# Up weights kept in DRAM, an earlier choice for the second half, and three shared jobs moved behind the routed ones

## Chip, cores and metric

The kernel runs on one core of one Trainium2 chip. The metric is the device time of one execution in microseconds (us). TensorE (PE) multiplies matrices; VectorE (DVE), ScalarE (ACT) and GpSimd (POOL) do the rest, and SyncE (SP) issues most DMAs.

## Reference

x has 32 sequences x 256 tokens x 128 channels, 8192 token rows in all. It goes through a mixture-of-experts layer, a retention layer and the same mixture of experts again:

```python
x = x + 0.5 * ffn(layernorm(x))          # called layer 1 below
x = x + attn(layernorm(x))               # retention, 16 heads
x = x + 0.5 * ffn(layernorm(x))          # called layer 2 below

def ffn(x):                              # xf: 8192 rows of 128
    shared = gelu(xf @ Wfc_s + bfc_s) @ Wproj_s + bproj_s        # hidden size 512
    probs = softmax(xf @ Wr)                                     # 8 experts
    topk_p, topk_i = top_k(probs, 2); topk_p /= sum(topk_p)
    routed = sum over e of gate[:, e] * (gelu(xf @ Wfc[e] + bfc[e]) @ Wproj[e] + bproj[e])
    return shared + routed
```

All is float32. The kernel multiplies in a faster format: each operand is split into a rounded part (`hi`) and the rest (`lo`), and three products hi*hi, hi*lo and lo*hi are summed.

## The kernel before

All 64 blocks of 128 token rows stay in SBUF (`x`). An expert layer works in two halves of 32 blocks. Rows are normalised into `xn`; logits and the two best experts of each row are found; each row gets a slot in `x_slots`, a buffer in DRAM sorted by expert.

**Jobs.** The matrix work is a list of 56 jobs per layer, each of 512 rows (`job_order`): first 16 shared jobs (no choice needed, rows straight from `xn`), then 20 routed jobs of half 0, then 20 of half 1. In each half 4 of the 20 are pair jobs, 256 rows for each of two experts. A position in this list is called job i; the code counts layers from 0. TensorE's program for job i (`tensor_jobs`) is `up(i)`, `turn(i+1)` (transposes of the next job's rows, L353), `back(i-2)` (y back to rows, L402), `down(i-1)` and then `tensor_between(i)`. ScalarE does y of job i-2, the four GELUs of job i, x_hi of job i+1 (`take_x`), the rows and the store of job i-2 (`take_rows`, L521), and `scalar_between(i)`. VectorE does x_lo of job i+1 (`split_x`), the update of x by job i-2 if it is shared, the two splits of h (`split_h`), and `vector_between(i)`. Each engine works its program strictly in this order.

**Choice and placing.** `choose_and_place` is a generator of small VectorE steps that ends in `slot` (L733). For half 0 it runs ahead of the jobs. For half 1 its steps are spread over jobs: `ROUTING_STEPS` says how many run at the end of which job. TensorE counts (`count_rows`, at job `COUNT_AT`) and places (`place_rows`, `PLACE_AT`) in between. Its work buffer `big1` for half 1 lies on the place of `xn`'s first blocks, so the choice waits until all scatters of half 0 are done and the early shared jobs have turned their rows.

**Scatter and gather.** GpSimd scatters the normalised rows of a half to `x_slots` (L847), 64 indirect DMAs per half, as soon as `slot` is there; between those of half 0 it computes the row scales (`row_scale`) of the second eight tiles. SP loads a routed job's rows into `xj` (L241) when all 64 scatters of its half have landed. The results go to `y_slots` (L521). When all 20 jobs of a half are stored, GpSimd gathers them, 64 indirect DMAs into a ring of 8 buffers (L859), and VectorE adds each to x (`combine`, L769): half 0's from the fourth job of half 1 on, four per job; half 1's in layer 1 during the retention, in layer 2 behind the last job (`remaining`).

**Weights.** The 9 experts' weights (expert 0 is the shared one) are split once, in layer 1: SP loads expert e into one of three stages, ScalarE rounds it (`round_weights`, L435, at job e+4), VectorE makes the rest (`split_weights`, L574, at job e+5). Both parts stay in SBUF as `w_hi` and `w_lo`, up and down weights. For each routed expert SP copies the up weights from there to one of three buffers `w_up`, with the expert number read from `table` (three DMAs, L254 and L256), and ScalarE copies the down weights (`place_down`, L480). The third up buffer and the second down buffer also lie on `xn`.

Of the kernel before, what the change touches and what calls it, by code (L numbers as in the profile page):

```python
# [14 lines left out]
ds = bass.ds  # L15
# [45 lines left out]
def job_order():  # L61
# [43 lines left out]
def ffn_programs(nc, m):  # L105

    sb, pb, sem = m["placed"]("ffn", m["region"]), m["bank"], m["sem"]
# [10 lines left out]
    w_up = [again("w_up2", [P, 2, HID], F32R)]
    w_down = [sb("w_down0", [P, 2, HID], F32R), again("w_down1", [P, 2, HID], F32R)]
    big_odd = again("big1", [P, 4 * JOB])  # L120
    w_up = [sb(f"w_up{i}", [P, 2, HID], F32R) for i in range(2)] + w_up
    big_even = m["placed"]("ffn_big", m["region"] + 4 * (BLOCKS * P + 6 * HID))("big0", [P, 4 * JOB])
# [7 lines left out]
    mv = [sb(f"mv{i}", [P, SUB, 2]) for i in range(2)]  # L130
    veps, rstd = sb("veps", [P, SUB]), [sb(f"rstd{i}", [P, SUB]) for i in range(2)]
    shifted = [sb(f"shifted{i}", [P, SUB]) for i in range(2)]
    logits = sb("logits", [P, HALF, NE])
    gap, egap1 = sb("gap", [P, BLOCKS]), sb("egap1", [P, BLOCKS])
    best = [sb(f"best{i}", [P, HALF]) for i in range(2)]
    number, total, counts = sb("number", [P, HALF]), sb("total", [P, NE]), sb("counts", [P, NE])
    parts_of, start, end = (sb(n, [P, 2, NE]) for n in ("parts_of", "start", "end"))
    first_slot, whole_slots, shift = (sb(n, [P, NE]) for n in ("first_slot", "whole_slots", "shift"))
    pairs, above = sb("pairs", [P, 2, NE, NE]), sb("above", [P, PAIR_JOBS])
    pad, over, slot_f = sb("pad", [P, 1]), sb("over", [P, ENTRIES]), sb("slot_f", [P, BLOCKS])  # L140
    expert, table = sb("expert", [P, ENTRIES]), sb("table", [P, 2 * ENTRIES], I32)

# [17 lines left out]
    w_hi_done, w_lo_done = sem("w_hi_done"), sem("w_lo_done")  # L160
    cleared, stored, preset = [sem(f"cleared{i}") for i in range(2)], sem("stored"), sem("preset")
# [43 lines left out]
    def sync_load(sp):  # L205
# [37 lines left out]
    def place_up(sp, job):  # L243

        sp.wait_ge(table_done, 2 * job["layer"] + job["half"] + 1)
        for at, s in enumerate(job["sets"]):
            e = sp.value_load(table[0:1, job["entry"] + at:job["entry"] + at + 1], min_val=1, max_val=NE)
            if s >= UP_SETS:
                sp.wait_ge(gelu_done, CH * (users[s - UP_SETS][0]["n"] + 1))
            if s % UP_SETS == 2:  # L250
                sp.wait_ge(scattered[0], norms_over(job["layer"])["scattered"])
                sp.wait_ge(x_turned, norms_over(job["layer"])["turned"])
            for i, part in enumerate((w_hi, w_lo)):
                sp.dma_start(w_up[s % UP_SETS][:, i, :].bitcast(F32), part[:, ds(e, 1), 0:HID].squeeze(1).bitcast(F32))\  # L254
                  .then_inc(up_ready[s % UP_SETS], 16)
            sp.dma_start(bias_up[s % UP_SETS][:], biases[:, ds(e, 1), 0:CH].squeeze(1)).then_inc(up_ready[s % UP_SETS], 16)  # L256
# [22 lines left out]
    def turn_rows(pe, layer, t):  # L279
# [10 lines left out]
        for j in range(SUB):  # L290
            last = pe.transpose(bank[:, j * P:(j + 1) * P], xn[:, SUB * t + j, :], ident)
# [19 lines left out]
    def place_rows(pe, q):  # L311
        chosen, ahead = chosen_of(q), ahead_of(q)
# [31 lines left out]
    def tensor_jobs(pe, layer):  # L344
        def turn(job):
# [5 lines left out]
            for j in range(SUB):  # L351
                rows = xj[job["ordinal"] % 2][:, j, :] if job["routed"] else xn[:, SUB * job["k"] + j, :]
# [1355 lines left out]
```

## Time and profile before

| | |
|---|---|
| median of three runs | 1582.1 us |
| lowest and highest | 1576.66 and 1582.23 us |
| profiled execution: span, first to last instruction | 1575.7 us |
| profiled execution: its own time | not given; the three runs are 1576.66, 1582.10 and 1582.23 us, 1.0 to 6.5 above the span |
| busy share of the span | PE 85%, DVE 69%, ACT 64%, POOL 59% |
| layer 1 | about 0 to 470 us |
| retention | about 470 to 1010 us |
| layer 2 | about 1010 to 1575.7 us |

Times in the profile are us from the span's start. A row of a timeline is one instruction or several alike; in brackets behind it is the idle time of its engine just before and what ended it. A row's L number is the line in the kernel.

### The profile page before, as it was taken

The page shows a single profiled execution, that of the slowest core. Times are in us where ns is not written, and L with a number is a line of the kernel's source. Part 1 is how long each engine was busy: PE and PEld are TensorE (multiplying, and loading weights), DVE is VectorE, ACT ScalarE, POOL GpSimd, SP SyncE. Part 2 cuts the span into 40 slices and gives each one's busy share as a digit, 9 for nine tenths or more (in the row PEclk, how much of TensorE's full clock was granted, in tenths as well). Part 3 has the DMA queues.
Part 4 walks back from the last instruction along what each step waited for, and adds up shares of the span by engine and source line. Part 5 has one row for each costly group of instructions (what it writes and reads, how often), then busy time and mean ns, then how long its engine had stood idle before and what let it go on. Part 6 is the DMA issues. An engine that isn't in the chain of part 4 may idle for free.

```text
span 1575.7 us, 31470 instructions
## 1 busy us (share of the span) xinstructions
PE 1340.2 (85%) x10776; PEld 1029.8 (65%) x10776; DVE 1094.3 (69%) x2296; ACT 1006.6 (64%) x1837; POOL 924.6 (59%) x744
## 2 busy tenths in 40 slices
PE   5799899969994999999999999669999996999700
PEld 5577778757873666666666666457777775877500
DVE  6777776647885888888777777567677854587622
ACT  1476578858882777777777777316657785788500
POOL 2388407744662588887556555516880478266576
PEclk9999999989996899999999999759999998999955
DMA  9513346646672564554444343000114663676522
GB/s 288 160 51 94 112 146 212 198 149 186 203 209 92 174 175 143 167 152 150 135 135 161 128 142 108 7 5 28 39 61 145 210 205 115 193 209 207 148 78 75
DMA packets 230592, 220.56 MB, mean 140 GB/s; under 512 B 32033, under 2 KB 173857, under 8 KB 230433
## 3 DMA queue, kind: packets, MB, share of 16 engines
q1 hardware_dynamic: 171808, 163.99, 32.7%
q0 software_dynamic: 16384, 33.59, 7.9%
q10 hardware_dynamic: 42240, 20.98, 4.8%
q8 instruction: 86, 1.41, 0.4%
q14 instruction: 74, 0.60, 0.1%
HBM read 81.96 MB, written 85.98 MB: 107 GB/s over the span
## 4 chain that ended last, share of the span: by engine, by line
PE 30%; POOL 13%; issue 11%; DVE 6%; ACT 6%; DMA 1%; ACTq 0%; SPq 0%; POOLq 0%; DVEq 0%
POOL x_slots L847 9%; PE psum L1047 5%; PE psum L1028 5%; PE psum L1062 4%; POOL ring L859 2%; ACT ret_absed L1197 2%; PE psum L1102 2%; PE psum L370 1%; DVE ret_f L1311 1%; PE psum L999 1%; PE psum L1094 1%; PE psum L372 1%; PE psum L371 1%; PE psum L389 1%; ACT ffn_h L492 1%
## 5 line engine op out<-in xcount | busy, mean ns | idle before, releaser
L847 POOL DMA_INDIRECT x_slots<-ffn_xn,slot x256 | 308.4, 1205 | 241.8 <-DVE slot L733 166.7
L859 POOL DMA_INDIRECT ring<-y_slots,slot x256 | 272.2, 1063 | 191.3 <-DMA y_slots<-ffn_y_rows 68.0
L787 DVE TENSOR_TENSOR ffn_h_lo<-ffn_h,ffn_h_hi 128x1024 fp32r<-128x1024 f32 x224 | 274.5, 1226 | 7.8
L492 ACT ACTIVATE ffn_h<-psum,ffn_bias_up 128x512 f32<-128x512 f32 (+1 forms) x384 | 215.0, 613 | 23.8 <-PE psum L372 18.3
L777 DVE TENSOR_TENSOR ffn_x_lo<-psum,ffn_x_hi 128x512 fp32r<-128x512 f32 x112 | 77.2, 689 | 178.0 <-ACT ffn_x_hi L465 177.9
L1457 POOL TENSOR_TENSOR ret_ssum<-ret_ssum,ret_power 128x32 f32<-128x32 f32 x32 | 174.3, 5447 | 42.8 <-DVE ret_ssum L1365 42.6
L1197 ACT ACTIVATE ret_absed<-ret_masked 128x1536 f32<-128x1536 f32 x128 | 190.0, 1485 | 1.5 <-PE psum L1062 0.4
L1341 DVE TENSOR_TENSOR ret_masked<-psum,ret_mask 128x512 f32<-128x512 f32 x256 | 174.4, 682 | 23.2 <-PE psum L1028 18.6
L1191 ACT ACTIVATE ret_masked<-psum 128x256 f32<-128x256 f32 x256 | 97.0, 380 | 105.4 <-DVE ret_masked L1341 105.0
L785 DVE CAST ffn_h_hi<-ffn_h 128x1024 fp32r<-128x1024 f32 x224 | 156.1, 697 | 4.1 <-PE psum L391 4.1
L769 DVE SCALAR_TENSOR_TENSOR x<-ring,gate,x 128x128 f32<-128x128 f32 x256 | 87.6, 352 | 78.0 <-DMA ring<-y_slots,slot 64.6
L1028 PE MATMUL psum<-ret_qk 32*128 32x128 f32 (+1 forms) x1024 | 128.1, 329 | 8.5 <-ACT ret_masked L1191 3.6
L492 ACT ACTIVATE ffn_h<-psum,biases 128x512 f32<-128x512 f32 x128 | 85.3, 689 | 46.2 <-PE psum L372 43.5
L1028 PEld LDWEIGHTS psum<-ret_qk 32*128 32x128 f32 x1024 | 77.6, 186 | 54.4 <-issue 33.7
L1062 PE MATMUL psum<-ret_absed,ret_pick 128*32 128x256 f32 (+1 forms) x2048 | 110.3, 333 | 0.0
L1047 PE MATMUL psum<-ret_masked,ret_v 128*32 128x256 f32 (+1 forms) x2048 | 109.8, 332 | 0.0
L465 ACT ACTIVATE ffn_x_hi<-psum 128x512 fp32r<-128x512 f32 x112 | 66.6, 595 | 67.0 <-PE psum L353 66.9
L508 ACT ACTIVATE ffn_xf<-psum,ffn_bias_down 128x512 f32<-128x512 f32 (+1 forms) x96 | 57.6, 617 | 67.0 <-PE psum L391 58.6
L370 PE MATMUL psum<-ffn_x_hi,ffn_w_up 128*128 128x512 f32 (+1 forms) x256 | 93.0, 363 | 7.6 <-DVE ffn_x_lo L777 5.2
L372 PE MATMUL psum<-ffn_x_hi,ffn_w_up 128*128 128x512 f32 (+1 forms) x256 | 90.3, 353 | 0.0
L371 PE MATMUL psum<-ffn_x_lo,ffn_w_up 128*128 128x512 f32 (+1 forms) x256 | 90.1, 352 | 0.0
L1047 PEld LDWEIGHTS psum<-ret_masked,ret_v 128*32 128x32 f32 x2048 | 53.6, 109 | 39.8 <-issue 5.6
(203 smaller groups left out, 3366.6 us busy)
## 6 DMA issues: line engine op xcount, KB each, us to landing
qk_copies<-ret_parts SPq DMA_DIRECT2D x128, 256.0 KB
ret_qk<-qk_copies SPq DMA_DIRECT2D x32, 1024.0 KB
ffn_xj<-x_slots SPq DMA_DIRECT2D x80, 256.0 KB
y_slots<-ffn_y_rows ACTq DMA_DIRECT2D x80, 256.0 KB
ffn_w_up<-w_hi SPq DMA_DIRECT2D x64, 256.0 KB
ffn_w_up<-w_lo SPq DMA_DIRECT2D x64, 256.0 KB
x_slots<-ffn_y_rows SPq DMA_DIRECT2D x40, 256.0 KB, 4.3
ffn_again_w_up<-w_hi SPq DMA_DIRECT2D x32, 256.0 KB
```

Of the source, the lines that this page charges most:

```text
L370: pe.matmul(bank, hi, x_hi[:, cols], start=True, stop=False)
L492: last = act.activation(to[:, cols], up_ps[c % UP_RING][:, cols], ACT.Gelu_apprx_tanh, bias=added[:, c:c + 1])
L785: dve.tensor_copy(h_hi[s][:], buf[:]).then_inc(hi_done, 1)
L787: dve.tensor_tensor(h_lo[s][:], buf[:], h_hi[s][:].bitcast(F32), ALU.subtract).then_inc(lo_done, 1)
L847: pool.indirect_dma_start(m["x_slot_rows"][half], slots_of(half, k), xn[:, half * HALF + k // 2, :], None)\
L859: pool.indirect_dma_start(ring[:, k % G_RING, :], None, m["y_slot_rows"][half], slots_of(half, k % BLOCKS))\
L1028: last = pe.matmul(out, k, q, start=True, stop=True)
L1047: last = pe.matmul(r_ps[rows, base + j * P:base + SEQ], values, src, start=(i == 0 and j == 0), stop=(i == 1 and j == 1))
L1062: last = pe.matmul(a_ps[rows, j * P:SEQ], one, absed[r % A_RING][:, quarter, cols], start=(r == 0 and j == 0), stop=(r == QUADS - 1 and j ...
L1197: act.activation(absed[q % A_RING][:], masked[q][:], ACT.Abs).then_inc(abs_done, 1)
L1341: dve.tensor_tensor(masked[p // 2][:, heads, 0:2 * P], s_ps[:, p % 2, :, P:3 * P], mask[:].unsqueeze(1).to_broadcast([P, 2, 2 * P]), ALU.m ...
L1457: pool.tensor_tensor(ssum[:], ssum[:], power[:], ALU.pow).then_inc(root_done, 1)
```

## The change

1. Up weights: when an expert is split, its up part goes to a small buffer (the two `w_down` buffers serve) and SP saves it to `up_rows` in DRAM with the biases behind each row (`sync_save`). A routed job's up weights come from there in one DMA. Only the down parts stay in SBUF.
2. The room pays for separate buffers: `big` alone, `const` and `ones` kept over the whole kernel, no buffer on `xn`'s first blocks. The waits of the choice, of the third up buffer and of the second down buffer on half 0's scatter go, and the second load of the constants goes.
3. The choice of half 1 starts at job 12 and has other steps per job.
4. In layer 2 the shared jobs 13, 14 and 15 stand behind the 40 routed ones.

```diff
-TURN_AT, SPLIT_AT, COUNT_AT, PLACE_AT = 3, 4, 16, 18
-ROUTING_STEPS = {14: 7, 15: 7, 17: 1, 19: 12, 20: 12, 21: 12}
+TURN_AT, SPLIT_AT, COUNT_AT, PLACE_AT = 3, 4, 14, 16
+ROUTING_STEPS = {12: 7, 13: 6, 15: 1, 17: 12, 18: 12, 19: 12}
+SHARED_FIRST = (TILES, 13)
+UP_ROW, UP_STRIDE = ROW + CH, ROW + 16
...
     for layer in range(2):
+        order = shared[:SHARED_FIRST[layer]] + routed_order + shared[SHARED_FIRST[layer]:]
...
+    w_up = [sb(f"w_up{i}", [P, UP_ROW], F32R) for i in range(UP_SETS)]
+    w_down = [sb(f"w_down{i}", [P, 2, HID], F32R) for i in range(2)]
+    up_out = w_down
...
+        sp.wait_ge(loaded_small, 48)
+        sp.dma_start(m["up_rows"][:, 1:, ROW:UP_ROW], biases[:, 1:, 0:CH]).then_inc(bias_saved, 16)
         for e in range(STAGES, EX):
             sync_weights(sp, e)
-        sp.wait_ge(w_lo_done, EX)
+            if e > STAGES:
+                sync_save(sp, e - STAGES)
+        for e in range(EX - STAGES, EX):
+            sync_save(sp, e)
+        sp.wait_ge(bias_saved, 16)
+        for i in range(2):
+            sp.wait_ge(up_saved[i], 16 * (NE // 2))
+
+    def sync_save(sp, e):
+        sp.wait_ge(w_lo_done, e + 1)
+        sp.dma_start(m["up_rows"][:, e, 0:ROW], up_out[e % 2][:].rearrange("p i n -> p (i n)").bitcast(F32)).then_inc(up_saved[e % 2], 16)
...
-            if s % UP_SETS == 2:
-                sp.wait_ge(scattered[0], norms_over(job["layer"])["scattered"])
-                sp.wait_ge(x_turned, norms_over(job["layer"])["turned"])
-            for i, part in enumerate((w_hi, w_lo)):
-                sp.dma_start(w_up[s % UP_SETS][:, i, :].bitcast(F32), part[:, ds(e, 1), 0:HID].squeeze(1).bitcast(F32))\
-                  .then_inc(up_ready[s % UP_SETS], 16)
-            sp.dma_start(bias_up[s % UP_SETS][:], biases[:, ds(e, 1), 0:CH].squeeze(1)).then_inc(up_ready[s % UP_SETS], 16)
+            sp.dma_start(w_up[s % UP_SETS][:].bitcast(F32), m["up_rows"][:, ds(e, 1), 0:UP_ROW].squeeze(1)).then_inc(up_ready[s % UP_SETS], 16)
...
     def round_weights(act, e):
         act.wait_ge(loaded_w[e % STAGES], 32 * (e // STAGES + 1))
-        act.activation(w_hi[:, e, :], stage[e % STAGES], ACT.Copy).then_inc(w_hi_done, 1)
+        if e > 2:
+            act.wait_ge(up_saved[e % 2], 16 * ((e - 1) // 2))
+        act.activation((up_out[e % 2] if e else up_shared)[:, 0, :], stage[e % STAGES][:, 0:HID], ACT.Copy)
+        act.activation(down_hi[:, e, :], stage[e % STAGES][:, HID:], ACT.Copy).then_inc(w_hi_done, 1)
...
     def split_weights(dve, e):
         dve.wait_ge(w_hi_done, e + 1)
-        dve.tensor_tensor(w_lo[:, e, :], stage[e % STAGES], w_hi[:, e, :].bitcast(F32), ALU.subtract).then_inc(w_lo_done, 1)
+        up = up_out[e % 2] if e else up_shared
+        dve.tensor_tensor(up[:, 1, :], stage[e % STAGES][:, 0:HID], up[:, 0, :].bitcast(F32), ALU.subtract)
+        dve.tensor_tensor(down_lo[:, e, :], stage[e % STAGES][:, HID:], down_hi[:, e, :].bitcast(F32), ALU.subtract).then_inc(w_lo_done, 1)
...
         if half:
-            dve.wait_ge(scattered[0], norms_over(layer)["scattered"])
-            dve.wait_ge(x_turned, norms_over(layer)["turned"])
             dve.wait_ge(slots_done, q)
-        else:
+        elif layer == 0:
             dve.memset(ones[:], 1.0)
-            dve.wait_ge(loaded_const, 16 * (layer + 1))
+            dve.wait_ge(loaded_const, 16)
...
-            ffn["sync_const"](sp)
...
-                first_gather = TILES + HALF_JOBS + 4
-                last_gather = TILES + JOBS + 3
+                first_gather = SHARED_FIRST[layer] + HALF_JOBS + 4
+                last_gather = SHARED_FIRST[layer] + JOBS + 3
```

`last_gather` is 59 in layer 1 and would be 56 in layer 2; with 56 jobs (0 to 55) no combine of half 1 runs inside the list of jobs before or after the change.

## Rows read from the trace of the kernel before

**Rows 1.** The page, busy tenths of TensorE in 40 slices of 39.4 us.

```profile
PE   5799899969994999999999999669999996999700
```

**Rows 2.** The page, the chain that ended last, shares of the span by line.

```profile
POOL x_slots L847 9%; PE psum L1047 5%; PE psum L1028 5%; PE psum L1062 4%; POOL ring L859 2%; ACT ret_absed L1197 2%; PE psum L1102 2%; PE psum L370 1%; DVE ret_f L1311 1%; PE psum L999 1%; PE psum L1094 1%; PE psum L372 1%; PE psum L371 1%; PE psum L389 1%; ACT ffn_h L492 1%
```

**Rows 3.** Timeline of PE: start, us, line, operation, idle before, releaser.

```profile
334.51 1.12 PE L353 MATMUL psum<-ident,ffn_xj 128*128 128x128 f32 x4 [13.02 <-DMA ffn_xj<-x_slots]
...
1163.21 0.60 PE L353 MATMUL psum<-ident,ffn_xn 128*128 128x128 f32 x4
...
1169.70 0.60 PE L353 MATMUL psum<-ident,ffn_xn 128*128 128x128 f32 x4
...
1179.24 0.66 PE L353 MATMUL psum<-ident,ffn_xj 128*128 128x128 f32 x4 [2.90 <-DMA ffn_xj<-x_slots]
...
1183.76 0.36 PE L370 MATMUL psum<-ffn_x_hi,ffn_w_up 128*128 128x256 f32 x1 [0.63 <-DMA ffn_bias_up<-biases]
...
1337.01 1.11 PE L353 MATMUL psum<-ident,ffn_xj 128*128 128x128 f32 x4 [15.18 <-DMA ffn_xj<-x_slots]
...
1471.56 0.60 PE L353 MATMUL psum<-ident,ffn_xj 128*128 128x128 f32 x4
...
1486.73 0.66 PE L402 MATMUL psum<-ident,ffn_xf 128*128 128x128 f32 x4 [0.78 <-ACT ffn_xf L508]
```

**Rows 4.** Stretches: length, busy (x) per engine, granted clock, DMA.

```profile
334.50:339.00 4.50, 4.49 (x17) 3.92 (x18) 0.95 (x2) 1.19 (x2) 1.10 (x1) 0.61 0.71 234
...
1337.00:1341.50 4.50, 4.49 (x15) 3.91 (x16) 0.69 (x1) 1.19 (x2) 1.42 (x1) 0.50 0.65 223
...
1490.60:1575.70 85.10, 0.00 (x0) 0.00 (x0) 22.64 (x64) 0.00 (x0) 61.25 (x64) 0.51 0.27 74
```

**Rows 5.** Timeline of POOL in layer 2.

```profile
1058.60 1.08 POOL L847 DMA_INDIRECT x_slots<-ffn_xn,slot  x1 [27.24 <-DVE slot L733]
...
1156.90 0.96 POOL L847 DMA_INDIRECT x_slots<-ffn_xn,slot  x1 [0.30 <-issue]
...
1173.42 1.67 POOL L847 DMA_INDIRECT x_slots<-ffn_xn,slot  x1 [0.30 <-issue]
...
1490.60 0.96 POOL L859 DMA_INDIRECT ring<-y_slots,slot  x1 [10.76 <-DMA y_slots<-ffn_y_rows]
...
1570.10 0.95 POOL L859 DMA_INDIRECT ring<-y_slots,slot  x1 [0.30 <-issue]
```

**Rows 6.** Timeline of DVE: the choice of half 1 in both layers.

```profile
235.38 0.20 DVE L733 CAST slot<-ffn_slot_f 128x64 uint32<-128x64 f32 x1
...
1180.57 0.69 DVE L777 TENSOR_TENSOR ffn_x_lo<-psum,ffn_x_hi 128x512 fp32r<-128x512 f32 x1 [0.66 <-ACT ffn_x_hi L465]
...
1191.58 0.16 DVE L640 COPY ffn_counts<-psum 64x8 f32<-64x8 f32 x1 [3.54 <-PE psum L308]
...
1206.64 0.17 DVE L646 COPY ffn_total<-psum 128x8 f32<-128x8 f32 x1 [3.31 <-PE psum L314]
...
1236.35 0.20 DVE L733 CAST slot<-ffn_slot_f 128x64 uint32<-128x64 f32 x1
```

**Rows 7.** Timelines of DVE, SP and ACT; DMA issues (KB, us to landing).

```profile
131.90 1.22 DVE L574 TENSOR_TENSOR w_lo<-ffn_stage_stage,w_hi 128x1024 fp32r<-128x1024 f32 x1
...
133.53 0.44 SPq L227 DMA_DIRECT2D ffn_stage_stage<-in_wproj  x1
...
134.05 1.05 ACT L435 ACTIVATE w_hi<-ffn_stage_stage 128x1024 fp32r<-128x1024 f32 x1
...
154.80 1.06 ACT L435 ACTIVATE w_hi<-ffn_stage_stage 128x1024 fp32r<-128x1024 f32 x1
...
ffn_stage_stage<-in_wproj SPq DMA_DIRECT2D x8, 256.0 KB, 3.5
```

**Rows 8.** Timelines of SP in layer 1, ACT queue in layer 2.

```profile
331.46 0.37 SPq L241 DMA_DIRECT2D ffn_xj<-x_slots  x1
...
1475.08 0.37 ACTq L521 DMA_DIRECT2D y_slots<-ffn_y_rows  x1
```

More of the change, by code:

```diff
@@ L105, in ffn_programs @@
 def ffn_programs(nc, m):
-    sb, pb, sem = m["placed"]("ffn", m["region"]), m["bank"], m["sem"]
+    keep, pb, sem = m["keep"], m["bank"], m["sem"]
+    stats = [keep(f"stats{i}", [P, SUB, 6]) for i in range(2)]
+    mv = [keep(f"mv{i}", [P, SUB, 2]) for i in range(2)]
+    veps, rstd = keep("veps", [P, SUB]), [keep(f"rstd{i}", [P, SUB]) for i in range(2)]
+    shifted = [keep(f"shifted{i}", [P, SUB]) for i in range(2)]
+    logits = keep("logits", [P, HALF, NE])
+    gap, egap1 = keep("gap", [P, BLOCKS]), keep("egap1", [P, BLOCKS])
+    best = [keep(f"best{i}", [P, HALF]) for i in range(2)]
+    number, total, counts = keep("number", [P, HALF]), keep("total", [P, NE]), keep("counts", [P, NE])
+    parts_of, start, end = (keep(n, [P, 2, NE]) for n in ("parts_of", "start", "end"))
+    first_slot, whole_slots, shift = (keep(n, [P, NE]) for n in ("first_slot", "whole_slots", "shift"))
+    pairs, above = keep("pairs", [P, 2, NE, NE]), keep("above", [P, PAIR_JOBS])
+    pad, over, slot_f = keep("pad", [P, 1]), keep("over", [P, ENTRIES]), keep("slot_f", [P, BLOCKS])
+    expert, table = keep("expert", [P, ENTRIES]), keep("table", [P, 2 * ENTRIES], I32)
+    m["region"] = -(-nc.sbuf_base // 32) * 32
+    sb = m["placed"]("ffn", m["region"])
     jobs = job_order()
@@ L118, in ffn_programs @@
[L118 to L122, printed above, removed]
+    const, ones, big = m["const"], m["ones"], m["big"]
+    xn_late = sb("xn_late", [P, HALF, P])
     h = [sb(f"h{i}", [P, 2 * JOB]) for i in range(4)]
-    const, ones = sb("const", [P, C_END]), sb("ones", [P, P])
+    staging = m["placed"]("ffn_stage", m["region"] + 4 * (HALF * P + 4 * 2 * JOB))
@@ L130, in ffn_programs @@
[L130 to L141, printed above, removed]
     x_hi, x_lo = sb("x_hi", [P, JOB], F32R), sb("x_lo", [P, JOB], F32R)
@@ L160, in ffn_programs @@
     w_hi_done, w_lo_done = sem("w_hi_done"), sem("w_lo_done")
+    up_saved, bias_saved = [sem(f"up_saved{i}") for i in range(2)], sem("bias_saved")
     cleared, stored, preset = [sem(f"cleared{i}") for i in range(2)], sem("stored"), sem("preset")
@@ L183, in up_weights_at @@
     def up_weights_at(s):
-        return 48 * (s // UP_SETS + 1)
-    def norms_over(layer):
-        return {"scattered": 16 * BLOCKS * (layer + 1), "turned": JOBS * layer + TILES * layer + HALF_TILES}
+        return 16 * (s // UP_SETS + 1)
     def gathers(layer, half):
@@ L351, in turn @@
             for j in range(SUB):
-                rows = xj[job["ordinal"] % 2][:, j, :] if job["routed"] else xn[:, SUB * job["k"] + j, :]
+                rows = xj[job["ordinal"] % 2][:, j, :] if job["routed"] else xn_rows(SUB * job["k"] + j)
                 last = pe.transpose(t_ps[:, j * P:(j + 1) * P], rows, ident)
@@ L360, in up @@
                 pe.wait_ge(up_ready[s % UP_SETS], up_weights_at(s))
-            weights = [(w_up[s % UP_SETS][:, 0, :], w_up[s % UP_SETS][:, 1, :]) for s in job["sets"]]\
-                or [(w_hi[:, 0, 0:HID], w_lo[:, 0, 0:HID])]
+            weights = [up_parts(s) for s in job["sets"]] or [(up_shared[:, 0, :], up_shared[:, 1, :])]
             for c in range(CH):
@@ L472, in place_down @@
                 act.wait_ge(w_lo_done, EX)
-            if s % 2:
-                act.wait_ge(scattered[0], norms_over(layer)["scattered"])
-                act.wait_ge(x_turned, norms_over(layer)["turned"])
+                act.wait_ge(up_saved[s % 2], 16 * (NE // 2))
             e = act.value_load(table[0:1, job["entry"] + at:job["entry"] + at + 1], min_val=1, max_val=NE)
@@ L877, in retention_programs @@
     x, ident = m["x"], m["ident"][:]
-    parts = sb("parts", [P, 2, 2, SEQ], F32R)
-    x_hi = [sb(f"x_hi{i}", [P, SEQ], F32R) for i in range(2)]
-    x_lo = [sb(f"x_lo{i}", [P, SEQ], F32R) for i in range(2)]
-    v = [sb(f"v{i}", [P, TB, PAIRS, 3, VD]) for i in range(2)]
-    r_turned = sb("r_turned", [P, TB * VB])
     mask = sb("mask", [P, 2 * P])
@@ L898, in retention_programs @@
     power = sb("power", [P, TB * HEADS])
+    v = [sb(f"v{i}", [P, TB, PAIRS, 3, VD]) for i in range(2)]
+    parts = sb("parts", [P, 2, 2, SEQ], F32R)
+    x_hi = [sb(f"x_hi{i}", [P, SEQ], F32R) for i in range(2)]
+    x_lo = [sb(f"x_lo{i}", [P, SEQ], F32R) for i in range(2)]
+    r_turned = sb("r_turned", [P, TB * VB])
     w_qk, w_vg = sums, f[:].rearrange("p k t -> p (k t)")
```

57 lines of the change are left out of this document (27 added, 30 removed).

## The prediction, as it went on record

> **What bounds the kernel now.** I read the 40 slices first [rows 1]: TensorE is at 9 tenths over most of the span and at 0 in the last two slices. The chain that ended last [rows 2] names the GpSimd scatters at L847 with 9% of the span, more than any TensorE line. So I looked at who waits at the borders of the stages [rows 3]: with the first routed job of a half, TensorE's transposes wait for the scattered rows of that half. At job 16 of layer 2 that is 2.9 us, at job 36 13.0 us in layer 1 and 15.2 us in layer 2. Around job 16 scatter and jobs are in balance; at job 36 the scatter of half 1 ends last. The last stretch [rows 4] has no matmul in 85.1 us: 64 gathers, started 1.262 us apart ((1570.10 - 1490.60) / 63, [rows 5]).
>
> So each routed layer is a chain: choice of half 0, 64 scatters of half 0, choice of half 1, 64 scatters of half 1, 20 routed jobs, 64 gathers. Shared jobs count only where they delay it or wait for it.
>
> **Layer 1: the choice starts at job 12, not 14.** Nothing at job 12 waits for half 0's scatter, since all 16 shared jobs still stand in front. Two shared iterations are 2 x 6.49 = 13.0 us (two turns of TensorE, [rows 3]). Two waits of VectorE go as well: the step that reads the counts now stands one iteration behind TensorE's count, and the total is read behind its matmul. Before, in layer 2, they waited 3.5 and 3.3 us [rows 6], and I take the same here: 6.9 us. Against it, jobs 12 and 13 also split the weights of experts 7 and 8, 1.2 us each [rows 7]: +2.4. Sum -17.5; the same instructions laid out one behind the other in program order give -17.9, which I take: slots ready at 217.7 instead of 235.6.
>
> *The saves.* Expert e's rounding (ScalarE, job e+4) now waits for the save of expert e-2, whose w_lo VectorE makes only in job e+3. For expert 5: the subtraction of expert 3 ends at 133.1, SP issues the load of expert 6 first, then the save, at 134.0; the rounding stood at 134.05 [rows 7]. A 256 KB load lands 3.5 us after issue, behind another one. The save is 512 KB behind 512 KB: between 3.5 us (no queueing) and 7.0 us (all in series), taken as 4.5, so 138.5. Behind the waiting instruction on ScalarE are y, four GELUs and the next x_hi, and for that waits VectorE. For experts 3 and 4 VectorE waits for GpSimd's row scales anyway, which hides most of it. From expert 5 on a loop over two iterations is left: rounding 1.2, y 0.7, GELUs 2.8, x_hi 0.6, VectorE's x_lo, update and h splits 4.9, weight split 1.3, two load issues 0.9, save 4.5: 16.9 us (durations as the costliest groups of the page give them), against 13.0 for two plain iterations. So expert 7's rounding comes at 155.4, and expert 8's at about 161.5 instead of 154.80. VectorE's job 13 comes 5.7 us later (ends: 2.5 and 10, the first with 3.5 us per save, the second with 7.0). That each weight operation is split into two adds about 0.2 us each and lies in that loop. [...] No row of before has a 512 KB save.
>
> The slots are then ready at 223.4, 12.2 earlier. The scatter took 95.9 us from there to its end [rows 6, 8], the last 10 of it with VectorE idle; now VectorE is busy all the time, which costs 8 scatters x (1.50 - 1.26) = 1.9 (the 1.50 is worked out below). So job 36's transposes start 10.3 earlier, at about 324. TensorE itself could be there at 322, so its wait shrinks to some 2 us and the slow clock behind it goes: after the 13.0 us wait the granted clock was 0.61 for 4.5 us, after the 15.2 us wait 0.50, which is the lower level of 1.2 GHz throughout [rows 4]. 4.5 x 0.39 = 1.8 more. Layer 1: **-12.1** (ends -15.5 and -8). It passes unchanged through the retention, which begins behind the last job.
>
> **Layer 2: three shared jobs behind the routed ones, choice at job 12.** Half 0's scatter is not made of shared jobs: GpSimd starts it at 1058.6 and ends it at 1175 either way [rows 5]. With 13 shared jobs TensorE has turned its last one at 1169.70 - 3 x 6.49 = 1150.2 and then waits some 20 us. What this gives: with VectorE idle from 1156 on, a scatter takes 1.26 us instead of (1173.42 - 1156.90) / 11 = 1.50 [rows 5], so 12 of them end some 3.2 us earlier. The Trainium skill ("SBUF — State Buffer", SBUF: two separate sides) says that GpSimd can't write descriptors while VectorE works in a mode that uses both ports; by that too only scatters beside an idle VectorE get shorter, and no other sum follows.
>
> What it doesn't give is the choice. VectorE begins job 12 with the x_lo of job 13, the first routed one, so the steps "at job 12" stand behind the end of scatter 0. Before: x_lo of job 16 at 1180.57, slots at 1236.55, 56.0 us and six iterations later [rows 6]. After: seven iterations from the x_lo of job 13, +6.5, and the first seven steps lie behind it, +3.6; the two waits, 3.5 and 3.3, go. 59.3 us: slots +3.3 relative to the scatter's end. And the 20 us wait lowers TensorE's clock, as at 1337: 4.5 x 0.50 = 2.3 [rows 4]. Job 33's start against job 36's before: -3.2 + 3.3 + 2.3 = **+2.4**. Half 1's scatter again ends last.
>
> *The end.* Before, it is 104.1 us from the last turn (job 55, 1471.56) to the span's end; the first gather starts at 1490.60, when the last job's store has landed [rows 3, 5]. After, jobs 33 to 52 take what 36 to 55 took, then come the turns of jobs 53 to 55: 6.7 + 6.5 + 6.5 = 19.7. The store that the gathers wait for is now job 52's. ScalarE issues it just behind the turn of job 55, as it issued job 53's at 1475.08 before, 3.5 us behind that turn [rows 8]; with 2 us to land it is there at turn + 5.5. VectorE's combines stand behind the loop: the last y is turned 15.2 us behind the last turn [rows 3], and the ring of 8 holds 8 x 1.5 = 12 us of gathers, so GpSimd hardly waits. End: 5.5 + 63 x 1.262 + 1.5 (the first gathers beside a busy VectorE) + 5.6 (last gather to the span's end) = 92.1. 19.7 + 92.1 - 104.1 = **+7.7**: 19.7 us of jobs stand in front of the end, and only 12 come back. Layer 2: **+10.1** (ends +6 and +14).
>
> **Up weights from DRAM.** Three DMAs per set become one, and two waits on half 0's scatter go, which were long over. I cost it at nothing: up loads run a job ahead, and only at a half's first job did TensorE wait for a set, 0.63 us in layer 2 [rows 3]; that may go or double. If the cover goes, each routed job pays (rival 4). The second load of the constants ended no wait.
>
> **Sum.** -12.1 + 10.1 = -2.0; 1575.7 (the span) - 2.0 = 1573.7. The median of the runs is 6.4 above the span: **1580**.
>
> **Rivals.** (1) The saves hide, landing in 3 us: layer 1 -17.5, and layer 2 at +8: 1573. Against it: a 256 KB load behind its like took 3.5. 0.17. (2) The shared jobs really fill the tail and layer 2 loses nothing: 1570. It needs the store of job 52 on its way 8 us earlier, for which nothing speaks, or both scatters at 1.26 us each. 0.11. (3) The saves cost more than I think: with 10 us from issue to landing the loop is 22 us, expert 8 some 18 us late, and layer 1 gives nothing: 1592. It decides from 7 us on; for it, GpSimd's scatter packets are on the same DMA engines. 0.16. (4) A set of up weights read from DRAM comes later than TensorE needs it: 0.3 us (half of the one wait seen) in each of the 40 routed jobs behind the two scatters that end last: 12, so 1592. It decides once a set needs longer than a job's 6.7 us to land; for it there is one short wait, against it all other jobs have none. 0.10. The forecast keeps 0.46.
>
> **Numbers.** 0.5% (7.9 us) is about what a measurement of this kernel can tell from no change. Faster: rivals 1 and 2, 0.28; same: 0.46; slower: 3 and 4, 0.26. The likeliest case's own range is 1574 to 1588 (layer 1 -15.5 to -8, layer 2 +6 to +14); with the rivals 1567 to 1592.
>
> **What the profile of the changed kernel would show.** Layer 1: slots 10 to 15 us earlier, TensorE's wait at job 36 under 5 us, roundings of experts 5 to 8 that wait for saves. Layer 2: a wait of some 20 us at job 13, another of 15 to 22 us at job 33, slots 63 us behind the scatter's end, about 92 us from the last turn to the end. I am wrong if the saves don't hold ScalarE, if VectorE's steps of job 12 run before the scatter of half 0 ends, or if the first gather of half 1 starts earlier than 5 us behind the last turn.

## The result, and the profile after

The changed kernel takes 1575.6 us (median of 20 runs, 1569.9 to 1578.2), the kernel before 1578.6 in the same runs (1576.3 to 1582.2). The ratio is 0.9976, 95% interval 0.9967 to 0.9985: within 0.5%, as forecast (1580, range 1567 to 1592). The profiled spans are 1572.1 and 1575.7 us.

Timeline of PE of the changed kernel, the rows that answer to [rows 3]: the first routed job of each half, and the last turn of layer 2, now that of a shared job.

```profile
328.64 0.69 PE L365 MATMUL psum<-ident,ffn_xj 128*128 128x128 f32 x2 [6.44 <-DMA ffn_xj<-x_slots]
...
1163.62 1.12 PE L365 MATMUL psum<-ident,ffn_xj 128*128 128x128 f32 x4 [19.06 <-DMA ffn_xj<-x_slots]
...
1329.30 1.12 PE L365 MATMUL psum<-ident,ffn_xj 128*128 128x128 f32 x4 [23.88 <-DMA ffn_xj<-x_slots]
...
1479.58 0.60 PE L365 MATMUL psum<-ident,ffn_xn_late 128*128 128x128 f32 x4
```

Timelines of DVE (slots of half 1 in both layers, x_lo of job 13) and of POOL (last scatter of half 0, first and last of half 1, first and last gather, layer 2), for [rows 5, 6].

```profile
224.27 0.19 DVE L740 CAST slot<-slot_f 128x64 uint32<-128x64 f32 x1
...
1165.40 0.69 DVE L784 TENSOR_TENSOR ffn_x_lo<-psum,ffn_x_hi 128x512 fp32r<-128x512 f32 x1 [21.88 <-ACT ffn_x_hi L479]
...
1228.46 0.19 DVE L740 CAST slot<-slot_f 128x64 uint32<-128x64 f32 x1
...
1158.55 0.95 POOL L854 DMA_INDIRECT x_slots<-xn_early,slot  x1 [0.30 <-issue]
...
1228.94 1.03 POOL L854 DMA_INDIRECT x_slots<-ffn_xn_late,slot  x1 [63.96 <-DVE slot L740]
...
1324.42 0.95 POOL L854 DMA_INDIRECT x_slots<-ffn_xn_late,slot  x1 [0.31 <-issue]
...
1484.01 0.95 POOL L866 DMA_INDIRECT ring<-y_slots,slot  x1 [17.62 <-DMA y_slots<-ffn_y_rows]
...
1566.40 0.95 POOL L866 DMA_INDIRECT ring<-y_slots,slot  x1 [0.30 <-issue]
```

What to see: slots of layer 1 came 11.1 us earlier (before: 235.38), its last turn 9.7 earlier (458.69 against 468.39). Layer 2's first slots, those of half 0, stand at 1046.95 against 1058.12, so all that lies ahead of them gave 11.2. From them to the span's end layer 2 takes 525.2 us; before, 517.6. -11.2 + 7.6 = -3.6, the difference of the spans. GpSimd stood idle for 63.96 us between the scatters of layer 2, waiting for slots.

### The profile page after: what moved, and what is told of

Its sections match the earlier page's. It is cut to its first block, busy times and chain, and to the rows that moved or that the text cites. A ratio compares the mean times of both kernels' runs of the same rounds, so it can differ in the third digit from the quotient of the medians.

```text
span 1572.1 us, 31133 instructions
## 1 busy us (share of the span) xinstructions
PE 1330.5 (85%) x10776; PEld 1030.9 (66%) x10776; DVE 1092.7 (70%) x2304; ACT 1002.6 (64%) x1846; POOL 927.7 (59%) x744
## 4 chain that ended last, share of the span: by engine, by line
PE 40%; POOL 12%; issue 7%; DVE 4%; ACT 3%; DMA 2%; ACTq 0%; POOLq 0%; DVEq 0%; SPq 0%
POOL x_slots L854 9%; PE psum L1035 7%; PE psum L1054 6%; PE psum L1069 6%; PE psum L1109 2%; POOL ring L866 2%; PE psum L1006 2%; PE psum L381 1%; ACT ffn_h L504 1%; PE psum L400 1%; PE psum L1080 1%; PE psum L402 1%; PE psum L401 1%; PE psum L1101 1%; PE psum L383 1%
## 5 line engine op out<-in xcount | busy, mean ns | idle before, releaser
L866 POOL DMA_INDIRECT ring<-y_slots,slot x256 | 277.6, 1084 | 185.5 <-DMA y_slots<-ffn_y_rows 76.2
L854 POOL DMA_INDIRECT x_slots<-ffn_xn_late,slot x128 | 157.8, 1233 | 151.5 <-DVE slot L740 113.1
L504 ACT ACTIVATE ffn_h<-psum,ffn_w_up 128x512 f32<-128x512 f32 (+1 forms) x384 | 214.6, 615 | 19.7 <-PE psum L383 16.0
L854 POOL DMA_INDIRECT x_slots<-xn_early,slot x128 | 149.9, 1171 | 90.3 <-DVE slot L740 53.6
L1198 ACT ACTIVATE ret_masked<-psum 128x256 f32<-128x256 f32 x256 | 96.9, 379 | 104.3 <-DVE ret_masked L1348 103.8
L381 PE MATMUL psum<-ffn_x_hi,ffn_w_up 128*128 128x512 f32 (+1 forms) x384 | 140.4, 366 | 14.9 <-DVE ffn_x_lo L784 12.7
L400 PE MATMUL psum<-ffn_h_hi,ffn_w_down 128*128 128x512 f32 (+1 forms) x384 | 143.7, 374 | 0.8 <-issue 0.8
L383 PE MATMUL psum<-ffn_x_hi,ffn_w_up 128*128 128x512 f32 (+1 forms) x384 | 136.9, 357 | 0.0
L402 PE MATMUL psum<-ffn_h_hi,ffn_w_down 128*128 128x512 f32 (+1 forms) x384 | 136.9, 357 | 0.0
L382 PE MATMUL psum<-ffn_x_lo,ffn_w_up 128*128 128x512 f32 (+1 forms) x384 | 136.9, 356 | 0.0
L401 PE MATMUL psum<-ffn_h_lo,ffn_w_down 128*128 128x512 f32 (+1 forms) x384 | 136.6, 356 | 0.0
```

The lines of the kernel that those rows point to most:

```text
L381: pe.matmul(bank, hi, x_hi[:, cols], start=True, stop=False)
L383: last = pe.matmul(bank, lo, x_hi[:, cols], start=False, stop=True)
L400: pe.matmul(y_ps[:, cols], hi, a_hi, start=(c == 0 and cols.start == 0), stop=False)
L504: last = act.activation(to[:, cols], up_ps[c % UP_RING][:, cols], ACT.Gelu_apprx_tanh, bias=added[:, c:c + 1])
L854: pool.indirect_dma_start(m["x_slot_rows"][half], slots_of(half, k), xn_rows(half * HALF + k // 2), None)\
L866: pool.indirect_dma_start(ring[:, k % G_RING, :], None, m["y_slot_rows"][half], slots_of(half, k % BLOCKS))\
```

## The experiments

All medians are beside runs of the kernel before on the same chip, but there were three chips: e1, e2, e4 and e5 (before: 1579.1 us), e6 to e9 (1580.2), e10 to e12 (1580.5). Across these groups the ratios compare better than the times. "Half 1" is the time from the turn of a layer's 21st routed job to 19 jobs later. The edits are shown abridged.

| kernel | us | ratio, 95% interval |
|---|---|---|
| weights in DRAM alone (e2) | 1573.9 | 0.9962 (0.9947 to 0.9977) |
| e2 and the early choice, no job moved (e1) | 1550.9 | 0.9826 (0.9811 to 0.9842) |
| the change: e1 and three jobs moved | 1575.6 | 0.9976 (0.9967 to 0.9985) |
| the change, three up transfers (e4) | 1571.1 | 0.9943 (0.9931 to 0.9956) |
| e4, up weights read from SBUF (e6) | 1580.2 | 1.0003 (0.9989 to 1.0016) |
| the change, two old waits back (e5) | 1576.6 | 0.9986 (0.9976 to 0.9996) |
| the change, old stride (e7) | 1575.8 | 0.9971 (0.9955 to 0.9987) |
| e1, third buffer for the saves (e8) | 1547.7 | 0.9794 (0.9771 to 0.9817) |
| e8, three up transfers (e9) | 1541.9 | 0.9761 (0.9737 to 0.9786) |
| e9, choice one job tighter (e10) | 1536.0 | 0.9734 (0.9713 to 0.9755) |
| the change, choice ahead of job 13 (e11) | 1545.2 | 0.9785 (0.9768 to 0.9802) |
| e10 and e11 together (e12) | 1530.8 | 0.9695 (0.9676 to 0.9713) |

### The change taken apart: e1 and e2

```diff
-SHARED_FIRST = (TILES, 13)
+SHARED_FIRST = (TILES, TILES)        # e1 and e2
-COUNT_AT 14, PLACE_AT 16, ROUTING_STEPS = {12: 7, 13: 6, 15: 1, 17: 12, 18: 12, 19: 12}
+COUNT_AT 16, PLACE_AT 18, ROUTING_STEPS = {14: 7, 15: 7, 17: 1, 19: 12, 20: 12, 21: 12}   # e2 too
```

> The changed kernel with all sixteen shared jobs of layer 2 ahead of its routed ones again; choice from job 12 and up weights in DRAM stay. Theory (the move of three shared jobs costs, the early choice pays in both layers): layer 2 loses the wait of 24 us ahead of its first routed job, its second slots come about 11 us earlier than before's against the first slots (178.2 us there), scatter 1 takes 95 us, the routed jobs of half 1 take 131 us as they do now, and the last turn stands about 104 us ahead of the span's end again instead of 92; the layer takes 502 to 508 us from its first slots instead of 525, and the kernel 1552 to 1562 us. Rival (the moved jobs fill time that is otherwise lost): 1578 us or more.

> The up weights in DRAM and the work buffer alone: choice steps at jobs 14 to 21 as in the kernel before, no job moved. Theory (the weights alone are about neutral: the saves hold ScalarE by some 5 us in layer 1 and scatter 1 runs some 5 us longer there, against some 7 us that the routed jobs of both second halves gain): 1580 us (1575 to 1585). Rival 1 (the weights in DRAM are the gain of this change): under 1573 us. Rival 2 (they are a loss that the earlier choice hides): over 1586 us. In every case the routed jobs of half 1 should take 130 to 131 us in both layers, if it is the weights that made them shorter.

Measured: 1550.9 us, just under the range of e1's theory, and 1573.9 us, between e2's theory and its rival 1. The 3 us between before and after are the sum of three large parts: weights in DRAM -5, the early choice -23, the moved jobs +25 us (1579.1, 1573.9, 1550.9, 1575.6, the last from its own comparison; by the ratios -6.0, -21.5 and +23.7). Timelines of e1, DVE (slots of half 1) and PE (jobs 16 and 36, last turn), layer 2:

```profile
1210.99 0.20 DVE L740 CAST slot<-slot_f 128x64 uint32<-128x64 f32 x1
...
1167.92 0.60 PE L365 MATMUL psum<-ident,ffn_xj 128*128 128x128 f32 x4
...
1314.39 0.90 PE L365 MATMUL psum<-ident,ffn_xj 128*128 128x128 f32 x3 [6.40 <-DMA ffn_xj<-x_slots]
...
1445.22 0.60 PE L365 MATMUL psum<-ident,ffn_xj 128*128 128x128 f32 x4
```

Counted from the layer's first slots (1050.04), half 1's slots stand at 161.0 us; with the moved jobs at 181.5 (1228.46 - 1046.95), before at 178.2. From the last turn to the end it is 103.9 us again. So the moved jobs cost 20.6 us at the slots, of which 18.0 reach half 1's first turn (264.4 against 282.4), and 7.7 in the tail: 25.7. With 0.4 more in half 1's jobs this is the difference of the two layers, 499.1 against 525.2 us from the first slots to the end.

For e2 my theory said 1580 and was too dear. The saves fall in jobs 7 to 12; with the choice at job 14 the slots of layer 1 come only 1.2 us later (236.58). Half 1 takes 131.3 and 130.5 us, before 133.9 and 134.6. That is what was expected if the weights are the cause. The profiled execution of e2 is its slowest (1577.1 us), so its trace doesn't show where all of the 5 us lie.

### Is it the choice behind job 13, or the place at the end? e11

TensorE counts and places half 1's rows of layer 2 ahead of job 13's transposes (and in layer 2 no longer at jobs 14 and 16), VectorE runs the whole choice ahead of job 13's x_lo:

```diff
             up(job)
+            if layer and i == 12:
+                count_rows(pe, 3)
+                place_rows(pe, 3)
             if i + 1 < len(mine):
                 turn(mine[i + 1])
...
+            if layer and i == 12:
+                for _ in routing:
+                    pass
             if i + 1 < len(mine):
                 split_x(mine[i + 1])
```

> The changed kernel with its three moved jobs; in layer 2 TensorE's count and placing stand ahead of the transposes of job 13, and VectorE runs the whole choice of half 1 ahead of the x_lo of job 13, in the time in which it waited for scatter 0 before. Theory (the moved jobs cost so much because the choice, bound to job numbers, moves behind scatter 0 with them): the choice takes 19 us as it does at the head of the layer (1027.8 to 1047.2), the slots stand at 1163 instead of 1228.5, scatter 1 no longer ends last, the wait of 24 us at job 33 is gone, and the kernel takes 1547 to 1553 us; the tail still costs its 7 to 8 us (112 us from the turn of job 52 to the end). Rival (the moved jobs cost by their place at the end, and the half's jobs then fill the time): 1565 us or more.

Measured: 1545.2 us, 30 less than the change and 2 below the theory's range. Timelines of e11: DVE (first and last step of the choice), POOL (last scatter of half 0, the power for the gates, first and last scatter of half 1), PE (jobs 33 and 52).

```profile
1144.54 0.42 DVE L622 COPY logits<-psum 128x256 f32<-128x256 f32 x1
...
1163.86 0.20 DVE L743 CAST slot<-slot_f 128x64 uint32<-128x64 f32 x1
...
1159.80 0.96 POOL L860 DMA_INDIRECT x_slots<-xn_early,slot  x1 [0.30 <-issue]
...
1160.78 5.87 POOL L864 TENSOR_TENSOR egap<-euler,gap 128x32 f32<-128x32 f32 x1
...
1166.85 1.03 POOL L860 DMA_INDIRECT x_slots<-ffn_xn_late,slot  x1 [0.20 <-issue]
...
1263.75 1.05 POOL L860 DMA_INDIRECT x_slots<-ffn_xn_late,slot  x1 [0.30 <-issue]
...
1300.79 0.60 PE L365 MATMUL psum<-ident,ffn_xj 128*128 128x128 f32 x4
...
1430.42 0.60 PE L365 MATMUL psum<-ident,ffn_xj 128*128 128x128 f32 x4
```

The choice takes 19.5 us while scatter 0 still runs, the second scatter starts 7.1 us behind the last of the first (the slots were ready before that; GpSimd was at the gates' power), and job 33's turn carries no wait. The tail stays: 111.5 us from job 52's turn to the end (1541.9 - 1430.4), against 103.9 without moved jobs. This settles it: the move's price was the choice that stood behind scatter 0, not the jobs' new place. It doesn't say that the choice is merely back where it was: e11's slots stand 115.2 us behind the layer's first ones, e1's 161.0, and so e11 comes out under e1 although its tail is longer.

### What the saves cost: e8

A third target for the split up weights, the gathers' ring, which is idle then:

```diff
-    up_out = w_down
+    up_out = [w_down[0][:], w_down[1][:], ring[:].rearrange("p (i a) c -> p i (a c)", i=2)]
-        if e > 2: act.wait_ge(up_saved[e % 2], 16 * ((e - 1) // 2))
+        if e > 3: act.wait_ge(up_saved[(e - 1) % 3], 16 * ((e - 1) // 3))
```

> The kernel without the moved jobs (1551 us), with a third buffer for the split up weights (the gathers' ring, idle then), so that a rounding waits for the save of three experts before. Theory (the saves hold ScalarE in jobs 9 to 13 of layer 1 by some 5 us, and with it VectorE's choice): the six waits of 0.4 to 4.3 us are gone or under 0.5 us, the second slots of layer 1 stand at 218 to 220 us instead of 224.5, and the kernel takes 1545 to 1547 us. Rival (they are idle time that costs nothing): 1550 to 1552 us.

Measured: 1547.7 us, 3.3 less than e1 (5 by the ratios, since the chips differ), just over the theory's range; slots of layer 1 at 220.68, 3.8 earlier. Waits of ACT from 115 to 165 us in e1 (us in total, times, longest); in e8 no rounding waits for a save there.

```profile
ACT ffn_w_down L448 <- DMA up_rows<-ffn_w_down: 15.3, 6, 4.0
```

Timelines of the changed kernel, SP (the save of expert 3, issued behind two loads) and ACT (roundings of experts 5, 7 and 8):

```profile
133.45 0.50 SPq L240 DMA_DIRECT2D up_rows<-ffn_w_down  x1
...
137.74 0.64 ACT L448 ACTIVATE ffn_w_down<-ffn_stage_stage 128x512 fp32r<-128x512 f32 x1 [2.37 <-DMA up_rows<-ffn_w_down]
...
154.22 0.64 ACT L448 ACTIVATE ffn_w_down<-ffn_stage_stage 128x512 fp32r<-128x512 f32 x1 [3.54 <-DMA up_rows<-ffn_w_down]
...
159.20 0.63 ACT L448 ACTIVATE ffn_w_down<-ffn_stage_stage 128x512 fp32r<-128x512 f32 x1 [0.44 <-DMA up_rows<-ffn_w_down]
```

Of 15.3 us of waits 3.8 reach the slots and 3.3 the end, in this pair of runs. The 3.8 is not firm: e9, below, runs the same program up to there, and in its profiled execution the slots stand at 223.74, only 0.8 earlier than in e1. The two part at one place. TensorE waits 1.8 us for ScalarE at 134.8 (e8) and 134.9 us (e9); from 135 to 145 us its granted clock is 1.00 in e8 and 0.66 in e9, and the next turn comes at 138.9 and 142.2 us.

### Why half 1's jobs became shorter: e4 to e7

Half 1 takes 130.1 and 131.2 us in the changed kernel, 3.8 and 3.4 less than before. My prediction had nothing there. Of each difference 2.8 us lie in one place: summed over 19 jobs, from the start of the transposes back (L402, now L413) to the start of the down products it is 11.0 and 10.9 us before, 8.2 and 8.1 after. Where the other 1.0 and 0.6 us lie is not shown. By the program the down products there need ScalarE's copy of the chosen down weights; the trace names no releaser for their short waits ("issue", 1.8 us in six waits in layer 1 before, 0.5 in one after). Groups by line in half 1 of layer 1, shapes apart: busy us and mean ns, then idle before them and its cause. Before:

```profile
L480 ACT ACTIVATE ffn_w_down<-w_hi 128x512 fp32r x11 | 7.0, 632 | 3.0 <-issue 2.9
L480 ACT ACTIVATE ffn_again_w_down<-w_hi 128x512 fp32r x10 | 6.3, 630 | 4.0 <-issue 4.0
```

After:

```profile
L492 ACT ACTIVATE ffn_w_down<-down_hi 128x512 fp32r x20 | 12.7, 633 | 1.4 <-issue 0.3
```

The copies themselves last as long (630 ns), but ahead of them 6.9 us of "issue" have become 0.3. Between the GELU and the copy ScalarE loads the expert's number from `table` into a register. Four candidates: the two waits that went, the address, the number of transfers, and their source.

```diff
# e5: ahead of every second set's copy
+    act.wait_ge(scattered[0], 16 * BLOCKS * (layer + 1))
+    act.wait_ge(x_turned, JOBS * layer + TILES * layer + HALF_TILES)
# e7: down_hi and down_lo as halves of one tensor
+    "down_parts": sb("down_parts", [P, EX, 2 * HID], F32R)
# e4: one transfer becomes three
+    for cols in (slice(0, HID), slice(HID, ROW), slice(ROW, UP_ROW)): sp.dma_start(w_up[...][:, cols], up_rows[:, ds(e, 1), cols])
# e6: e4 with SBUF as the source, the bias from SBUF too
+    for cols, part in ((slice(0, HID), down_hi), (slice(HID, ROW), down_lo)): sp.dma_start(w_up[...][:, cols], part[:, ds(e, 1), :])
```

> The changed kernel with each up load as three transfers (high part, low part, bias) instead of one, all still from DRAM. Theory (ScalarE's copies of the down weights made the second halves' jobs shorter): nothing changes, 1573 to 1578 us, second halves at 130 and 131 us. Rival (one transfer instead of three did it): second halves at 133 to 134 us again, 1580 to 1583 us.

> The changed kernel with the two waits that the kernel before had ahead of every second set's copy of the down weights on ScalarE (on scatter 0 and on the eighth tile's turn, both long met). Theory (instructions of ScalarE's queue ahead of the copies made the second halves' jobs longer): the odd sets' copies start some 0.2 us later, and the second halves take 1 to 3 us more each: 1577 to 1581 us. Rival (the waits are free): 1573 to 1578 us, second halves at 130 and 131 us.

> The run with three transfers for each up load (1571 us), with the weights taken from SBUF: its transfers read the chosen expert's down weights (same size and shape, high and low part) instead of the up weights in DRAM, and the bias in SBUF, so the routed jobs multiply by the wrong weights; their number, order and sizes stay. Theory (taking the up weights from DRAM is what shortened the jobs of the second halves, since transfers no longer read SBUF beside the engines): the second halves take 133 to 134 us again, 3 to 4 us more each, and the kernel 1577 us or more. Rival (the source is free; the copy of the down weights is what changed): second halves stay at 129 to 130 us, and the kernel within 2 us of 1571.

> The changed kernel with the down weights' high and low parts in one tensor of 1,024 elements an expert, the stride that the kernel before had, instead of two tensors of 512. Theory (the address of a copy that a register chooses costs ScalarE more with the longer stride): the copies start some 0.3 us later after the GELU, the down products of a job wait for them again (11 us between the transposes of a row of 20 jobs and their down products, now 8), and each second half takes 3 us more: 1580 us. Rival (the stride is free): 1573 to 1578 us, 8 us, second halves at 130 and 131 us.

Group of the copies of the high part, e6:

```profile
L494 ACT ACTIVATE ffn_w_down<-down_hi 128x512 fp32r x20 | 12.6, 629 | 7.7 <-issue 7.7
```

In e6 7.7 us of issue are back, the stretch is 10.6 us long and half 1 of layer 1 takes 134.6 us (e4: 130.0); 1.6 us of that is one wait of TensorE for a bias. In layer 2, which chooses other experts in e6 because layer 1's weights are wrong, the stretch is 10.5 us, and half 1 132.4 against 128.9. The kernel takes 9 us more than e4: e6's theory holds. In e4, e5 and e7 the same group has 0.5, 0.7 and 0.5 us of issue. e5's two waits lengthen the stretch by 0.4 and 0.8 us but leave 1576.6 us, and with the old stride the stretch is 8.2 and 8.0 us and the kernel at 1575.8: both hold to their rival. So it is the source: with up weights read from SBUF, ScalarE comes later to a copy that a register chooses. Two things stay open: which of ScalarE's instructions in between is the slow one, and whether any source in SBUF does it, since both the kernel before and e6 load from the very tensors that ScalarE copies from.

e4 disagreed with both its theories: three transfers are 4.5 us better than one. Waits of ACT in the changed kernel, then in e4:

```profile
ACT ffn_y_rows L531 <- DMA y_slots<-ffn_y_rows: 8.1, 9, 2.2
```

```profile
ACT ffn_y_rows L532 <- DMA y_slots<-ffn_y_rows: 1.3, 3, 0.8
```

`y_rows` is a single buffer; its next eviction waits for the last store, and this store of 256 KB lands later beside one load of 514 KB than beside parts of it. The sums vary between kernels but don't overlap: 3.7 to 8.1 us in the seven with one load, 0.9 to 2.6 in the four with three. Scatter 1 of layer 1 takes 98.9 us in the changed kernel and 96.3 in e4. That the loads' size does both is shown; through which queue, and how much of the 4.5 us each gives, is not.

### Better kernels: e9, e10, e12

```diff
-COUNT_AT 14, PLACE_AT 16, ROUTING_STEPS = {12: 7, 13: 6, 15: 1, 17: 12, 18: 12, 19: 12}
+COUNT_AT 13, PLACE_AT 15, ROUTING_STEPS = {12: 13, 14: 1, 16: 12, 17: 12, 18: 12}    # e10
```

> As the run before, and each up load as three transfers. Theory (a large up load holds up the scatters, the rows' store and the y rows behind it on the same queues, three smaller ones less): 2 to 5 us less than with one transfer, so 1541 to 1545 us; scatter 1 of layer 1 takes some 2.5 us less. Rival (that gain came from the late first turn of the moved order alone): the same as the run before within 1 us.

> The run with the third buffer and three transfers (1542 us), with the choice one job tighter: 13 steps at job 12, the count at 13, placing at 15, the 36 steps left at jobs 16 to 18. Theory (scatter 1 still ends last in both layers, so each microsecond of the slots counts until TensorE's waits of 5.3 and 5.1 us at job 36 are gone): slots 6 to 8 us earlier in both layers, waits at job 36 under 1 us, no slow clock behind them, and 10 to 12 us less: 1530 to 1533 us. Rival (the denser steps make VectorE the bound of these jobs): 1537 us or more.

> The tighter choice, the third buffer and three transfers, with the three jobs moved and the whole choice in the wait, as in the run before. Theory: layer 1 as in the tighter run; in layer 2 no scatter ends last at half 1, so its length is 117 us to job 13's transposes, some 136 us of jobs, 129 us of jobs and 112 us of tail, 494 us from its first slots, against 490 us without the move: 1532 to 1537 us, 2 to 5 us more than the tighter run. Rival (the moved jobs pay once the choice is not behind them, since TensorE's wait of scatter 0 goes): less than the tighter run.

e9: 1541.9 us, scatter 1 of layer 1 96.3 us against 99.9; the theory's time holds, and the gain of 5.7 is a little over its 2 to 5. e10: 1536.0. The slots moved as expected in layer 1 (216.57, 7.2 earlier) and by 3.8 in layer 2, counted from its first slots, and the waits at job 36 are gone in both; but in layer 2 the denser steps at job 12 bring job 16 later, 122.5 us from the first slots instead of 119.0, and eat most of what the wait gave: TensorE waits 2.4 us for their end ahead of its count, and behind that its granted clock is 0.54 for 7 us (1149 to 1156). It lies between theory and rival. Timeline of PE of e10, the count of layer 2:

```profile
1149.15 1.50 PE L323 MATMUL psum<-ones,big 128*64 128x1 f32 x16 [2.35 <-DVE big L638]
```

e12: 1530.8 us (1529.2 to 1534.0), under all runs of e10 (1534.3 to 1539.8): here my theory falls and the rival holds. From the first slots of layer 2: 116.1 us to job 13's turn, 135.4 to job 33, 127.5 to job 52, 111.5 to the end, 490.5; e10 needs 122.5 to job 16, 140.7, 127.3 and 103.8, 494.2. The steps that lengthened e10's jobs lie in e12 inside a wait: half 1's first turn stands at 251.4 us from the first slots instead of 263.2, and these 11.8 us are more than the tail's 7.7. e12 is 3% faster than the kernel before.

## Why the prediction was right

The number held, and so did the mechanism in its main lines: layer 1 gains, layer 2 loses, half 1's scatter ends last, and the tail keeps 7.5 us of the moved jobs (7.7 forecast). That the sum came so close (-2.0 forecast, -3.6 between the spans) is in part luck, since errors of both signs cancelled.

| part | forecast | measured |
|---|---|---|
| layer 1, to half 1's first turn | -10.3 | -5.9 |
| layer 1, half 1's jobs (forecast: the clock) | -1.8 | -3.8 |
| from layer 1's last turn to layer 2's first slots | 0 | -1.5 |
| layer 2, to half 1's first turn | +2.4 | +3.5 |
| layer 2, half 1's jobs | 0 | -3.4 |
| end | +7.7 | +7.5 |

- **Slots of layer 1.** Forecast 223.4, measured 224.3. Without the saves 217.7 forecast, 220.7 measured in e8 and 223.7 in e9: the earlier choice gives 14.7 or 11.6, not 17.9, and the saves cost 3.8 or 0.8, not 5.7. The loop of saves was right in each turn: roundings of experts 5, 7 and 8 forecast at 138.5, 155.4 and 161.5, measured at 137.7, 154.2 and 159.2. The save took 4.3 us (133.45 to 137.74), forecast 4.5. Experts 3 and 4 waited as well.
- **Scatter 1 of layer 1.** Mis-sized: +1.9 forecast, +5.6 measured (98.9 us against 93.3). Before, VectorE worked in 53 of the 63 intervals between scatters, now in 59; such an interval took 1.52 us and now takes 1.59, and one beside an idle VectorE 1.26 as before. The six more explain 1.5 us, the longer intervals 4. So TensorE's wait at job 36 stayed at 6.4 us, over the 5 forecast, and the 1.8 us of clock didn't come back: granted clock 0.60 in the 4.5 us behind it, 0.61 before. Stretches of the changed kernel behind jobs 36, 13 and 33:

```profile
328.60:333.10 4.50, 4.46 (x17) 3.89 (x18) 0.91 (x2) 1.20 (x2) 1.45 (x1) 0.60 0.96 282
1163.60:1168.10 4.50, 4.48 (x15) 3.90 (x16) 1.29 (x2) 0.60 (x1) 1.38 (x1) 0.50 0.91 273
1329.30:1333.80 4.50, 4.50 (x18) 3.97 (x19) 1.21 (x2) 1.20 (x2) 1.55 (x1) 0.67 0.94 285
```

- **Up weights from DRAM "at nothing".** Wrong by 7 us in the kernel's favour: half 1's jobs -3.8 and -3.4 (e6). Rival 4 never showed: in the changed kernel no routed job waited for a set.
- **Scatter 0 of layer 2.** -3.2 forecast, -3.7 measured (1047.44 to 1158.55 is 111.1 us, before 114.8); the forecast's own working, 12 x (1.50 - 1.26), gives 2.9. The wait at job 13 is 19.1 us, forecast 20. VectorE is idle from 1143.5 us on, and the last 11 intervals are 1.26 us long. The Trainium skill ("SBUF — State Buffer", SBUF: two separate sides) says that GpSimd can't write descriptors while VectorE works in a mode that uses both ports, and the trace agrees in so far as intervals were longer only while VectorE worked; its modes no row shows.
- **Slots behind x_lo of job 13.** 59.3 us forecast, 63.1 measured, 55.8 before. Of the difference some 1.4 us are the slow clock, which the forecast had as a term of its own (2.3): the granted clock is 0.50 until 1168.1, 2.7 us behind x_lo. The rest is that I took off 6.8 us for two waits of VectorE. Stretches from job 16 (before) and job 13 (after) to the slots:

```profile
1180.00:1237.00 57.00, 53.46 (x310) 43.83 (x307) 44.42 (x77) 40.74 (x86) 1.61 (x2) 1.00 0.47 151
```

```profile
1164.00:1229.00 65.00, 62.29 (x346) 51.22 (x344) 51.77 (x89) 46.62 (x96) 1.04 (x2) 0.97 0.53 160
```

  TensorE is busy 94% and 96% of them and VectorE 78% and 80%, so TensorE sets the pace. The two waits are gone from the trace, but an iteration did not get shorter to match: 55.8 us for seven iterations before, 63.1 for eight after, 8.0 and 7.9 each. At the slots this makes +7.0 where +3.3 and part of the clock's +2.3 were forecast, and TensorE waits 23.9 us at job 33, forecast 15 to 22.
- **The end.** 19.7 and 92.1 us forecast, 19.1 and 92.5 measured. The first gather starts 4.4 us behind the last turn, earlier than the 5 that I had set as a limit; the gathers then take 82.4 us instead of 81.0, so the sum hardly moves.
- **From span to median.** I added 6.4 us, from three runs; with 20 runs the median stands 2.9 above the span. 1573.7 and 2.9 would have been 1576.6. The low end of the likeliest case's range, 1582.1 - 15.5 + 6, is 1572.6 and not 1574.

The -1.5 us between the layers can't be the change's doing: that stretch varies by 4 us between runs (last section).

The prediction saw that the choice stands behind scatter 0 in layer 2 and booked it at 3.3 us. It compared with the kernel before, in which the choice begins at job 14, and so never asked what the early choice gives without the move: 23 us over both layers, nearly as much as the move cost in layer 2 alone.

## What to carry to other kernels

Where work of one stage is tied to job numbers of another, moving jobs moves that work too: ask what it would do in the wait that the move opens, before pricing the jobs. A wait of an engine that does not set the pace may be worth nothing when it goes, as VectorE's two waits here; read the pacing engine's busy share over the stretch first. One profiled execution can differ from the next of the same program by as much as a small term of the sum (slots of layer 1 at 220.7 and 223.7 us), so such a term needs more than one trace. When several edits of one change have opposite signs, run each alone: here -5, -23 and +25 us looked like no change.

## What the hardware showed unexpectedly

- Reading the up weights from SBUF instead of DRAM delays ScalarE ahead of its register-chosen copies by 0.3 to 0.4 us each (6.9 us for 21 sets and 7.7 for 20, with DRAM 0.3 to 0.7 in all). Both kernels that show it read the tensors that ScalarE copies from.
- One load of 514 KB held back a store of 256 KB on another queue: 8.1 us of waits, 1.3 with the load in three parts; the kernel was 4.5 us faster with more transfers.
- A scatter beside an idle VectorE takes 1.26 to 1.27 us in every kernel. Beside a working VectorE it took 1.52 to 1.61 us on average, by kernel and layer (scatter 1). With one large load from DRAM scatter 1 of layer 1 took 98.9 (the change) and 99.9 us (e8), with three parts 96.3 both times (e4, e9); what else moves it is open.
- TensorE's clock behind the same short wait need not be the same: behind 1.8 us without work at 135 us its granted clock stayed at 1.00 in e8 and was 0.66 over the next 10 us in e9, which cost 3.2 us by the next turn. What decides it is open.
- The time from layer 1's last turn to layer 2's first slots, the same work in all, was 589.7 us before, 588.3 after, and 587.3 (e5) to 591.8 (e9) in the others: a difference of up to some 4 us between spans says nothing of an edit.
